# Loading parameters and contexts in five parts over two queues in place of three

## The reference

```
def _L0_xattn_ref(teacher_logits, teacher_features, Wq, bq, Wk, bk):
    query = jnp.einsum('bnc,dc->bnd', teacher_features, Wq) + bq
    key = jnp.einsum('bnc,dc->bnd', teacher_features, Wk) + bk
    energy = jnp.einsum('bnd,bmd->bnm', query, key)
    attention = jax.nn.softmax(energy, axis=-1)
    x_m = jnp.einsum('bln,bmn->blm', teacher_logits, attention)
    return x_m
...
x = x + jnp.tanh(g_xattn[0]) * _L0_xattn_ref(_layernorm(x, axis=-1), ctx_1024, ...)
x = x + jnp.tanh(g_ffn[0]) * _L0_ffn_ref(_layernorm(x, axis=-1), w_gating, w_linear)
```

## Time and profile before

| What | us |
|---|---|
| median of 3 runs | 50.27 |
| lowest and highest | 49.81, 50.54 |
| the profiled execution's own time | 49.62 |
| its span, first to last instruction | 47.8 |
| PE busy | 41.6 (87%) |
| DVE busy | 35.6 (74%) |
| ACT busy | 29.3 (61%) |
| POOL busy | 16.9 (35%) |

### The profile page before, as it was taken

One profiled execution on the slowest core, in us unless ns is written; L12 is line 12 of the kernel. 1 busy time (PEld: TensorE's weight loads), 2 busy tenths in 40 slices (PEclk: granted clock), 3 DMA queues, 4 the chain that ended last, 5 costly groups with the idle time before them and its releaser, 6 DMA issues.

```text
span 47.8 us, 843 instructions
## 1 busy us (share of the span) xinstructions
PE 41.6 (87%) x246; PEld 28.4 (60%) x246; DVE 35.6 (74%) x110; ACT 29.3 (61%) x67; POOL 16.9 (35%) x35
## 2 busy tenths in 40 slices
PE   3997999956999999998999999999999999994300
PEld 1316788816788888843447665566567688862000
DVE  0101689999797989799999972987666998899900
ACT  0903937597996999374797869744448933572000
POOL 3203995069899260600600530000000895006000
PEclk9999999999999999999999999999999999999999
DMA  0499999999999930000000000000000035300092
GB/s 0 66 368 358 329 394 382 234 198 177 111 106 103 105 33 0 0 0 21 0 0 0 0 0 0 0 7 0 0 0 0 0 123 196 133 0 0 0 341 98
DMA packets 3460, 4.64 MB, mean 97 GB/s; under 512 B 384, under 2 KB 2176, under 8 KB 3456
## 3 DMA queue, kind: packets, MB, share of 16 engines
q1 hardware_dynamic: 2448, 3.61, 21.9%
q0 software_dynamic: 864, 0.79, 17.6%
q10 hardware_dynamic: 144, 0.20, 1.3%
HBM read 5.90 MB, written 1.05 MB: 145 GB/s over the span
## 4 chain that ended last, share of the span: by engine, by line
PE 65%; DVE 13%; DMA 9%; SPq 3%; ACT 2%; issue 1%; DVEq 1%
PE bank L633 15%; PE bank L639 14%; PE bank L658 14%; PE bank L593 14%; DMA x_sb<-x 9%; DVE st L407 4%; PE bank L565 4%; DVE nmax L414 2%; PE bank L615 2%; PE bank L558 2%; SPq L208 2%; DVE aq L474 2%; DVE mv L410 1%; DVE attn L425 1%; ACT xq L341 1%
## 5 line engine op out<-in xcount | busy, mean ns | idle before, releaser
L465 DVE SCALAR_TENSOR_TENSOR ap<-bank,gl 128x512 f16<-128x512 f32 (+1 forms) x20 | 11.6, 582 | 3.5 <-issue 1.6
L350 ACT ACTIVATE gl<-bank 128x512 bf16<-128x512 f32 (+1 forms) x20 | 10.0, 508 | 6.0 <-PE bank L633 6.0
L658 PE MATMUL bank<-wl,aq 128*128 128x256 fp8e4 x64 | 10.1, 273 | 0.7 <-DVE aq L474 0.6
L633 PE MATMUL bank<-xq,wg 128*128 128x512 fp8e4 (+1 forms) x40 | 10.2, 337 | 0.2 <-ACT xq L341 0.2
L639 PE MATMUL bank<-xq,wg 128*128 128x512 fp8e4 (+1 forms) x40 | 10.2, 337 | 0.0
L658 PEld LDWEIGHTS bank<-wl,aq 128*128 128x128 f16 x64 | 6.0, 98 | 4.1 <-DVE aq L474 1.6
L593 PE MATMUL bank<-attnT,xT_sb 128*128 128x256 f32 x32 | 8.1, 386 | 0.0
L474 DVE TENSOR_SCALAR aq<-ap 128x512 uint16<-128x512 uint16 (+1 forms) x20 | 6.6, 334 | 0.0
L278 POOL TENSOR_TENSOR yo<-ys,x 128x256 f32<-128x256 f32 x4 | 2.9, 747 | 9.3 <-ACT ys L358 9.3
L593 PEld LDWEIGHTS bank<-attnT,xT_sb 128*128 128x128 f32 x32 | 5.6, 190 | 0.7 <-ACT attnT L324 0.2
L263 POOL TENSOR_TENSOR r<-ve,neg_half 128x2 f32<-128x2 f32 x4 | 3.0, 758 | 8.5 <-DVE ve L448 8.5
(11 more groups left out here) (50 smaller groups left out, 53.8 us busy)
## 6 DMA issues: line engine op xcount, KB each, us to landing
x_sb<-x SPq DMA_DIRECT2D x4, 256.0 KB, 4.4
xT_sb<-xT SPq DMA_DIRECT2D x4, 256.0 KB, 6.2
out<-yo SPq DMA_DIRECT2D x6, 128.0 KB, 2.0
wg<-w_gating POOLq DMA_DIRECT2D x4, 128.0 KB, 8.1
par<-params_ctxT SPq DMA_DIRECT2D x1, 256.0 KB, 3.4
wl<-w_linear POOLq DMA_DIRECT2D x2, 128.0 KB, 10.3
out<-yo SPq DMA_DIRECT2D x1, 256.0 KB, 2.0
par<-params_ctxT SPq DMA_DIRECT2D x1, 194.0 KB, 3.1
```

The source lines that it names most:

```text
L350: nc.scalar.activation(gl[:, s % 2, toks], gate_b[s % 2][:, toks], ACT.Gelu_apprx_tanh).then_inc(gelu_ready, 1)
L465: nc.vector.scalar_tensor_tensor(ap[:, s % NAP, toks], up_b[s % 2][:, toks], ACT_SCALE, gl[:, s % 2, toks], ALU.mult, ALU.mult).then_inc(p ...
L633: mm = nc.tensor.matmul(gate_b[s % 2][:, toks], wg8[:, c, k, 0, o:o + P], xq[:, g, k, toks], start=(k == 0), stop=(k == KC - 1))
L658: mm = nc.tensor.matmul(halves(y_b[g][i])[:, t], aq[:, s % NAQ, m:m + P], wl8[:, j], start=(j == 0 and t == 0), stop=(j == HT - 1), skip_g ...
```

## The change

`CUTS` gets two more cuts: the loads are now columns 0 to 132 (query weight, biases, gates; 66 KB), 132 to 388 (context 0; 128 KB), 388 to 516 (key weight; 64 KB), 516 to 772 (context 1; 128 KB) and 772 to 1284 (contexts 2 and 3; 256 KB). The tensor's layout is as before. SP issues loads 0, 2 and 4, ACT issues 1 and 3. `project_q` waits for loads 0 and 1 in batch 0, for 3 in batch 1 and for 4 in batches 2 and 3; `project_k(0)` waits for load 2. The text of POOL's wait on `s_ctx[1]` is unchanged, but that semaphore now belongs to the load of context 0. The wait of ACT on `s_ctx[0]` now is for the 66 KB load.

```diff
--- before.py
+++ after.py
@@ -53,7 +53,7 @@
     LAG = 3
     EPS = 1e-5
     WARM_UP = 6
-    CUTS = (0, P + 4 + L, NPAR + 2 * L, NPAR + 4 * L)
+    CUTS = (0, P + 4, P + 4 + L, NPAR + L, NPAR + 2 * L, NPAR + 4 * L)
     SPLIT = 4
 
 
@@ -203,7 +203,7 @@
 
         @block.sync
         def _(sp):
-            for c in (0, 2):
+            for c in (0, 2, 4):
                 cols = slice(CUTS[c], CUTS[c + 1])
                 sp.dma_start(par[:, cols], params_ctxT[:, cols]).then_inc(s_ctx[c], 16)
             for b in range(B):
@@ -297,8 +297,9 @@
 
         @block.scalar
         def _(act):
-            cols = slice(CUTS[1], CUTS[2])
-            act.dma_start(par[:, cols], params_ctxT[:, cols]).then_inc(s_ctx[1], 16)
+            for c in (1, 3):
+                cols = slice(CUTS[c], CUTS[c + 1])
+                act.dma_start(par[:, cols], params_ctxT[:, cols]).then_inc(s_ctx[c], 16)
             act.wait_ge(s_ctx[0], 16)
             nc.scalar.activation(tg[:, :], gates, ACT.Tanh).then_inc(gates_ready, 1)
 
@@ -535,8 +536,9 @@
                 nc.tensor.matmul(turn_b[0][:, :], ones[:, 0:P], ones, start=True, stop=True)
 
             def project_q(b):
-                if b != 1:
-                    pe.wait_ge(s_ctx[min(b, 2)], 16)
+                if b == 0:
+                    pe.wait_ge(s_ctx[0], 16)
+                pe.wait_ge(s_ctx[(1, 3, 4, 4)[b]], 16)
                 if b >= 2:
                     pe.wait_ge(q_ready, b - 1)
                 nc.tensor.matmul(q_b[b % 2][:, 0:L], wqT, cT(b), start=True,
@@ -544,7 +546,7 @@
 
             def project_k(b):
                 if b == 0:
-                    pe.wait_ge(s_ctx[1], 16)
+                    pe.wait_ge(s_ctx[2], 16)
                 if b >= 2:
                     pe.wait_ge(k_ready, b - 1)
                 nc.tensor.matmul(k_b[b % 2][:, 0:L], wkT, cT(b), start=True,
```

## The result

The changed kernel takes 51.14 us in the median (50.99 to 51.36, 4 runs), the kernel before 50.15 (49.81 to 50.54, 4 runs). The ratio is 1.0199 with a 95% interval from 1.0112 to 1.0287: slower by about 2%, where a change too small to measure was forecast. Some executions of every kernel are over 1.5% longer than its fastest: all ratios compare the others alone, and the profiled executions of e4, f5, f6, g4 and i3 were long ones. The profiled execution took 50.99 us with a span of 49.2; the one before, 49.62 with 47.8. Between these two, 1.37 us have to be found; the medians are 0.99 apart.

The account below looks back on a forecast made before the run. The prediction took the landing of x, not the parameters, to bound the start. Its only nonzero term, +0.16 us for packets, on 49.62 gave 49.78, or 50.43 against the median; it forecast 50.4, range 49.8 to 51.0.

Parts of the forecast that it names:

- What bounds the kernel: Start of the kernel: the landing of x, then DVE's work to the first attention turn at 11.15 us, not the parameters.
- the 1.41 us of slack: Before DVE's first row maximum: energies lie ready 1.41 us, from 6.76 to 8.17, before DVE takes them.
- Step 1: PE's first projection: query 0 starts 0.37 us earlier, near 3.5, energy 0 ends near 6.4; worth nothing on the path.
- Step 2: SP's queue: one more load issued ahead of x delays its issue; taken as 0, bounds 0 and +0.43 us.
- Step 3: DMA engines: 288 more, smaller packets delay x of batch 1 by 0.16 us; range 0 to 0.53.
- The price of a packet: DMA engines: about 0.009 us of engine time a packet, beside about 37 us a MB, from two stretches of SP's queue.
- upper end of 0.53: DMA engines: most that packets could delay x, in us, if limited by packet rate rather than bytes.
- rival D: Early DMA queues: each added load pays a thin start of 0.6 us, +1.36 in all, 51.6; chance 0.05.
- Steps 4 and 5: ACT's table load moves from 1.15 to about 1.55, hidden, 0; POOL's loads start half a microsecond sooner, taken as 0.
- Rivals C and E: C: batch 1's 0.22 us wait goes, 50.05, chance 0.15; E: PE idles, clock falls to 1.2 GHz, 52.0, chance 0.05.

Follow-up runs that it names:

- e4: The kernel before, with POOL's weight loads waiting until x of batch 1 has landed; ratio to the kernel before 0.996.
- f5: The changed kernel's five loads, but SP issues only 0 and 4, ACT 1, 2 and 3; ratio to the kernel before 1.017.
- f6: The kernel before, with PE's first projection also waiting for its load 2 (contexts 2 and 3); ratio 1.002.
- g4: The kernel before with three loads cut at columns 132 and 772, so the first is 66 KB; ratio 0.9997.
- i3: The kernel before, with ACT's table load also waiting for the identity matrix; ratio 0.998.
- g3: The kernel before, with SP issuing x of batches 0 and 1 ahead of contexts 2 and 3; 49.69 us, ratio 0.984.
- f2: The kernel before with only the first cut added: four loads, SP issuing 0 and 3, ACT 1 and 2; ratio 1.0145.
- h1: The kernel before with three loads, ACT's load split into 400 packets, 256 more, in one transfer; ratio 0.9985.
- e1: The changed kernel, with POOL's weight loads waiting for context 1 in place of context 0; ratio to the kernel before 1.020.
- i1: The changed kernel's five loads, but ACT issues only load 1, SP 0, 2, 3 and 4; ratio to the kernel before 1.014.
- h2: The kernel before, with loads 0 and 1 each issued in two halves of 64 partitions, five transfers; ratio 1.042.
- e2: The kernel before, with POOL's wait taken away so its weight loads wait for nothing; ratio 1.120.
- f1: The changed kernel, with PE's first projection also waiting for load 4 (contexts 2 and 3); one counting run, 52.34 us, no ratio.
- g1: The changed kernel, with SP issuing the transposed x only once x of batch 1 has landed; ratio to the kernel before 1.026.
- g2: The kernel before, with SP issuing the transposed x only once x of batch 1 has landed; ratio 1.013.
- e3: The changed kernel, with POOL's weight loads waiting until x of batch 1 has landed; two counting runs, 50.98 and 51.05 us, no ratio.
- h3: The kernel before with x of batches 0 and 1 ahead of contexts 2 and 3, and four loads, query weight split off; ratio 1.037.

## Why the prediction was wrong

**What bounds the kernel** was read rightly as far as the direction of this change goes: with x of batch 0 landing 1.7 us later, the first row maximum and everything behind it moved by 1.37. The other direction was not as free as the 1.41 us of slack suggest: g3 brings x 0.72 us sooner and its profile gains 0.04, since PE, at half rate for its first matmuls, then sets the time.

**Step 1** held for query 0, at 3.34 (I said 3.5), and in that it was worth nothing. It failed for energy 0, which I had ending near 6.4 and which ended at 7.23, later than before (6.76). PE went on from the warm-up without a pause and stayed at half rate: query 0 took 1.19 us for the two against 0.70 before, which is the 1.2 GHz level, though the column of the granted clock reads 1.00; the pair at 5.77 was the first at the full rate. The late x hid that.

**Step 2**, the issue of x 0.46 us later, is not the loss: f2 and f5 issue x at the old time and lose 1.5 and 1.7% all the same.

**Step 3 failed.** "More and smaller packets" was the wrong unit, and its upper end of 0.53 was taken from stores late in the kernel, a stretch that had small packets but not several loads just issued. The price of a packet was, if anything, too high: h1 adds 256, and its ratio doesn't reach the 0.15 us. The loss goes with the number of transfers into which the bytes ahead of x are cut:

| Transfers of parameters and contexts, x behind them | Kernels | Ratio | Runs that count |
|---|---|---|---|
| 3 | e4, f6, g4, h1, i3 | 0.996, 1.002, 1.000, 0.9985, 0.998 | 9, 3, 5, 9, 5 of 10 |
| 4 | f2 | 1.0145 | 4 of 4 |
| 5 | the change, e1, f5, i1 | 1.020, 1.020, 1.017, 1.014 | 4, 4, 3, 3 of 4 |
| 5, four of them of half the partitions | h2 | 1.042 | 4 of 4 |

Kernels in which POOL, PE or the transposed x was moved at a price of its own (e2, f1, g1, g2) are left out, and e3, which has no ratio. At unchanged bytes more transfers are also smaller ones. g4 shows that one small load costs nothing, but no run changes the number at a fixed size, so number and size aren't told apart.

In place of +0.16 the term measures +1.37 between the profiled executions (0.99 between the medians), and the first row maximum moved by 1.37, past the 0.5 that I had named as the sign of being wrong. That is by chance the price of rival D, and its test, x of batch 1 landing after 7.4, came true (7.6). Its mechanism did not: D had each load pay a thin start, and the first 1.6 us were no thinner than before. I gave it 0.05, since x on one queue at full share seemed to speak against it; that row shows few transfers following one another, not five issued within 1.3 us.

The Trainium skill, "DMA: Bandwidth & Descriptors", section Bandwidth, told against small DMAs, with figures for transfers that GpSimd issues, while these came from SP and ACT. The trace agrees on the direction for the number of transfers, but not on the reason given there, descriptors: h1 has 400 packets for 144 in the same bytes and no loss, and g4 has a 66 KB load and none.

**Steps 4 and 5** held: the table load (i3) and POOL's earlier start (e1) cost nothing that the ratios show. **Rivals C and E** did not occur: no gain came, and the matmuls behind 12.5 us run as before (the first feed-forward pair takes 0.60 us in both), though PE had idled 1.84 us ahead of them, more than E asked for.

**What stays open** is why two more transfers make packets stall from about 3.2 us on. The stalls begin within half a microsecond of the first landings (3.0 to 3.2 us in the change), and the kernel before has a weaker dip at 4.5 to 5.0, also after its first landings (3.8). h1 speaks against a simple link: its first load had landed by 3.3 us, and the engines went on at 383 and 365 GB/s. Nor is a late x confined to more transfers: in the profiled executions of e4, f6, g4 and i3, kernels with three, DVE took x of batch 1 only at 7.33 to 7.98 (6.43 in the kernel before). So the change may make frequent what happens now and then without it. The Trainium skill, "DMA: Bandwidth & Descriptors", section Queues, rings and completion order, says that the write of a transfer's signal lands only after every earlier write of that engine, over all its queues; more signals early on could so hold engines up. That is an argument, and no run here shows it.

## What to carry to other kernels

Before splitting a load so that its first part comes sooner, ask what stands behind it on the queue and whether that is what the chain begins with. Here the parts that came sooner had time to spare, and the first added transfer cost 0.7 us (f2) and the second 0.3 more, on the load that had none. Reordering the transfers at an unchanged number (x ahead of the contexts wanted last) gained 1.6% against the runs beside it, of which the two profiled executions show next to nothing (0.04 us).

## What the runs showed that I had not expected

Two transfers more of the same bytes took the DMA engines from about 400 to about 200 GB/s for the stretch from 3.2 to 4.0 us (141 to 219 in seven kernels of five transfers, 50 in i1; with four, 286 in f2 and 374 in h3), while 256 packets more in one transfer left it at 383. Weight loads issued by POOL from 1.7 us on took the traffic from 4.5 to 5.0 down to 47 GB/s and cost 12%. Query 0 ran at half rate in the changed kernel (at 3.34 us) and in g3 (at 3.67), and at the full rate in the kernel before (at 3.87), while the column of the granted clock reads 1.00 in all three.
